# A fused two-layer block on one core: the last steps of the attention and the norms behind it rearranged

## The reference, cut to what matters

```python
def _L1_xattn_ref(x, context, mask, g_norm, null_kv, Wq, Wkv, Wout, g_out):
    ...                      # q, k, v of 16 heads of 64; one null key and value in front
    sim = jnp.einsum('bhid,bhjd->bhij', q, k)
    ...
    attn = jax.nn.softmax(sim.astype(jnp.float32), axis=-1).astype(sim.dtype)
    out = jnp.einsum('bhij,bhjd->bhid', attn, v)
    out = out.transpose(0, 2, 1, 3).reshape(b, -1, INNER)
    out = out @ Wout
    return layer_norm(out, g_out)

def _act_fake_quant(x, clip_factor):
    scale = jax.nn.sigmoid(clip_factor) * jnp.max(jnp.abs(x)) / QMAX
    return jnp.clip(_ste_round(x / scale), -QMAX - 1.0, QMAX) * scale
...
x = x + jnp.tanh(g_xattn[1]) * _L1_xattn_ref(_layernorm(x, axis=-1), ctx_768, ...)
x = x + jnp.tanh(g_ffn[1]) * _L1_ffn_ref(_layernorm(x, axis=-1), L1_ffn_clip_x, ...)
```

## Time and profile before

| what | value |
|---|---|
| time, median of 3 runs | 330.18 us (328.82 to 331.27) |
| the profiled execution: its own time | 329.04 us |
| the profiled execution: its span, first to last instruction | 327.2 us |
| busy in that span: PE, PEld | 301.6 us (92%), 245.2 us (75%) |
| busy in that span: DVE, ACT, POOL | 240.8 us (74%), 230.5 us (70%), 173.9 us (53%) |
| mean granted TensorE clock | 0.99 of full speed |

### The profile page before, as it was taken

The page is one execution under the profiler, slowest core; times in us unless marked ns, Lnnn a source line. Parts: engine busy times, 40 slices in busy tenths (PEclk is TensorE's granted clock), DMA queues, the critical chain, the costliest instruction groups (busy, mean ns, idle before and its releaser), DMA issues.

```text
span 327.2 us, 7975 instructions
## 1 busy us (share of the span) xinstructions
PE 301.6 (92%) x2682; PEld 245.2 (75%) x2682; DVE 240.8 (74%) x723; ACT 230.5 (70%) x781; POOL 173.9 (53%) x301
## 2 busy tenths in 40 slices
PE   6779999999999869999999999999999998977595
PEld 6557668686767658898998988989888777743375
DVE  3887999999885456666777787777777686547865
ACT  2776596969899677877878778787787774319190
POOL 3115616252443145458889797895957849245100
PEclk9999999999999999999999999999999999979989
DMA  5671010002020000000000000000000000000004
GB/s 148 164 205 26 1 26 1 1 2 66 3 62 3 0 0 2 2 2 2 2 3 2 1 4 2 2 0 3 3 2 1 2 3 1 2 0 1 2 0 130
DMA packets 12649, 7.22 MB, mean 22 GB/s; under 512 B 3969, under 2 KB 12161, under 8 KB 12609
## 3 DMA queue, kind: packets, MB, share of 16 engines
q1 hardware_dynamic: 11728, 6.51, 7.2%
q10 hardware_dynamic: 880, 0.20, 0.3%
HBM read 5.66 MB, written 1.05 MB: 20 GB/s over the span
## 4 chain that ended last, share of the span: by engine, by line
PE 73%; DVE 8%; issue 7%; ACT 7%; POOL 4%; DVEq 0%; POOLq 0%; ACTq 0%
PE psum L1084 14%; PE psum L1220 10%; PE psum L1517 9%; PE psum L1531 7%; PE psum L1088 7%; PE psum L1090 6%; PE psum L1089 6%; PE psum L1099 2%; ACT work L1025 2%; DVE hgm L2149 2%; PE psum L1632 2%; PE psum L1540 1%; PE psum L1095 1%; DVE work L2008 1%; PE psum L1317 1%
## 5 line engine op out<-in xcount | busy, mean ns | idle before, releaser
L1025 ACT ACTIVATE work<-psum,nmx 128x129 f32<-128x129 f32 x256 | 83.4, 420 | 25.9 <-DVE nmx L2014 24.8
L603 POOL TENSOR_TENSOR work<-work,rden 128x512 f32<-128x512 f32 x64 | 66.4, 1038 | 0.0
L2014 DVE TENSOR_REDUCE nmx<-psum 128x4 f32<-128x516 f32 x64 | 41.5, 689 | 29.4 <-PE psum L1220 29.3
L1084 PE MATMUL psum<-ident,work 128*128 128x128 f32 (+2 forms) x376 | 58.4, 281 | 3.9 <-DVE work L2008 2.6
L1025 ACT ACTIVATION_READ_ACCUMULATOR work<-psum,nmx 128x1 f32 x256 | 58.7, 229 | 0.0
L1088 PE MATMUL psum<-split 128*128 128x256 f32 (+2 forms) x128 | 52.0, 406 | 1.5 <-issue 0.8
L1084 PEld LDWEIGHTS psum<-ident,work 128*128 128x128 f32 (+2 forms) x376 | 41.7, 142 | 13.1 <-issue 3.3
L2008 DVE COPY work<-psum 128x512 f32<-128x512 f32 x64 | 43.9, 686 | 7.8 <-PE psum L1084 4.9
L1090 PE MATMUL psum<-split 128*128 128x256 f32 (+2 forms) x128 | 43.3, 338 | 0.0
L1089 PE MATMUL psum<-split 128*128 128x256 f32 (+2 forms) x128 | 43.2, 338 | 0.0
L1220 PE MATMUL psum<-KT,work 64*128 64x129 f32 x512 | 37.5, 285 | 2.5 <-DVE den L2024 1.8
(11 more groups left out here) (209 smaller groups left out, 576.6 us busy)
## 6 DMA issues: line engine op xcount, KB each, us to landing
KT<-in_L_xattn_Wkv SPq DMA_DIRECT2D x2, 384.0 KB, 5.2
X<-in_x SPq DMA_DIRECT2D x1, 768.0 KB, 6.8
out_x<-X SPq DMA_DIRECT2D x3, 256.0 KB, 2.3
work<-in_ctx SPq DMA_DIRECT2D x3, 192.0 KB, 2.6
KT<-in_L_xattn_Wout SPq DMA_DIRECT2D x1, 512.0 KB, 4.7
work<-in_L_xattn_Wq SPq DMA_DIRECT2D x1, 512.0 KB, 3.6
work<-in_L_xattn_Wout SPq DMA_DIRECT2D x1, 512.0 KB, 4.0
X<-in_x SPq DMA_DIRECT2D x1, 256.0 KB, 3.3
```

The lines of the kernel that those rows point to most:

```text
L603: pool.tensor_tensor(sx_[:, :, 0:S], sx_[:, :, 0:S], bcast(rden[n % 2][:, :], S), ALU.mult).then_inc(p_ready.sem, 1)
L1025: ins = act.activation(Sx[n % 4][:, j, :], psum[:, here, (j // 2) * K1:(j // 2 + 1) * K1], ACT.Exp, bias=nmx[n % 2][:, j:j + 1], accum_out ...
L1084: return pe.transpose(dst, src, ident[0:m, 0:m])
L2014: dve.tensor_reduce(nmx[n % 2][:, :].rearrange("p (c a) -> p c a", a=2), sim, AX_X, ALU.max, negate=True).then_inc(max_done.sem, 1)
```

## The change

The loops of all four engines now end with round 32 (`NR`), and what is left is written out behind them. Numbers of the steps below are 62 (`NS - 2`) and 63 (`NS - 1`), of the pairs 6 (`NPAIR - 2`) and 7.

- Step 63 is normalised on VectorE (`last_normalise`) in place of GpSimd. It signals with semaphores of its own.
- Its transposes go to bank 6, and ScalarE copies them out (`last_p_evac`); its values go to the second half of bank 0. The copies of the values out of banks 5 and 0 are two (`last_o_evac`), each of half the columns.
- TensorE runs both groups of transposes first, then both halves of `out_proj(30)`.
- The last pair's `y_evac` is gone: `last_statistics` and `last_centred` read bank 7. `last_centred` subtracts the mean and multiplies with the gain in one instruction for each sequence, and `last_output` multiplies with the reciprocal deviation and adds the residual in another.
- On GpSimd `y_affine(6)` stands behind `normalise(62)` in place of before it. On VectorE the next norm of pair 6 stands behind `y_aggregate(7)`, and its maximum behind `x_aggregate(7)`.
- The first run of `keep_clock_long` has 24 matmuls in place of 36.

The core of the diff, with one line of context; the new semaphores and three of the four loop headers are left out:

```diff
...
@@ -364,3 +366,2 @@
         X_STATS_AT, X_AGGR_AT, RSTD_X_AT, XN4_AT, GM_AT = 9, 10, 10, 11, 12
-        LAST = RPP * (NPAIR - 1) + GM_AT
 
@@ -659,8 +660,8 @@
             pool.wait_ge(setup_a.sem, setup_a.at(9))
-            for m in range(LAST + 1):
+            for m in range(NR + 1):
                 if 9 <= m < 21 and m % 2 == 1:
                     down_weights((m - 9) // 2)
-                if in_rounds(m - 1):
-                    normalise(2 * (m - 1))
-                    normalise(2 * (m - 1) + 1)
+                for n in (2 * (m - 1), 2 * (m - 1) + 1):
+                    if 0 <= n < NS - 1:
+                        normalise(n)
                 t = pair_at(m, RSTD_Y_AT)
@@ -668,6 +669,8 @@
                     rstd_y(t)
-                    if t < NPAIR - 1:
+                    if t < NPAIR - 2:
                         y_affine(t)
                 t = pair_at(m, X3_AT)
-                if t is not None and t < NPAIR - 1:
+                if t is not None:
+                    if t == NPAIR - 2:
+                        y_affine(t)
                     y_gain(t)
@@ -680,2 +683,5 @@
                     split_x(t + 2)
+            rstd_x(NPAIR - 2)
+            rstd_y(NPAIR - 1)
+            rstd_x(NPAIR - 1)
 
...
@@ -1045,2 +1051,19 @@
 
+
+            def last_p_evac():
+                act.wait_ge(pt_done.sem, pt_done.at(NS))
+                act.wait_ge(ot_done.sem, ot_done.at(NS - 2))
+                act.activation(PTs[(NS - 1) % 2], bank[6], ACT.Copy).then_inc(pt_last.sem, 1)
+
+            def last_o_evac(h):
+                act.wait_ge(ot_done.sem, ot_done.at(NS - 1 + h))
+                act.wait_ge(wo_done.sem, wo_done.at(NS - 2))
+                act.activation(oT[:, 2 * h * S:2 * (h + 1) * S], bank[(5, 0)[h]][:, 2 * h * S:2 * (h + 1) * S],
+                               ACT.Copy).then_inc(ot_out.sem, 1)
+
+            last_p_evac()
+            pn_evac(NPAIR - 1)
+            last_o_evac(0)
+            last_o_evac(1)
+
             def x_quantised(f):
@@ -1500,7 +1523,11 @@
             def p_transposes(n):
-                pe.wait_ge(p_ready.sem, p_ready.at(n + 1))
-                if n >= 1:
-                    pe.wait_ge(pt_out.sem, pt_out.at(n))
+                if n < NS - 1:
+                    pe.wait_ge(p_ready.sem, p_ready.at(n + 1))
+                    if n >= 1:
+                        pe.wait_ge(pt_out.sem, pt_out.at(n))
+                else:
+                    pe.wait_ge(p_last.sem, p_last.at(1))
+                    pe.wait_ge(q_out.sem, q_out.at(RPP * NPAIR))
                 for j in range(HPU):
-                    ins = transpose(bank[4][:, j * S:(j + 1) * S], Sx[n % 4][:, j, 0:S])
+                    ins = transpose(bank[4 if n < NS - 1 else 6][:, j * S:(j + 1) * S], Sx[n % 4][:, j, 0:S])
                 ins.then_inc(pt_done.sem, 1)
@@ -1510,5 +1537,10 @@
                 b, hg = unit(n)
-                pe.wait_ge(pt_out.sem, pt_out.at(n + 1))
+                if n < NS - 1:
+                    pe.wait_ge(pt_out.sem, pt_out.at(n + 1))
+                else:
+                    pe.wait_ge(pt_last.sem, pt_last.at(1))
                 if n >= 2:
                     pe.wait_ge(ot_out.sem, ot_out.at(n // 2))
+                    if n == NS - 1:
+                        pe.wait_ge(den_done.sem, den_done.at(NS - 1))
                 for j in range(HPU):
@@ -1516,3 +1548,3 @@
                     at = (n % 2) * 2 * S + (j // 2) * S
-                    ins = pe.matmul(bank[5][rows, at:at + S], V[:, b, HPU * hg + j, :],
+                    ins = pe.matmul(bank[5 if n < NS - 1 else 0][rows, at:at + S], V[:, b, HPU * hg + j, :],
                                     PTs[n % 2][:, j * S:(j + 1) * S], start=True, stop=True)
@@ -1522,3 +1554,3 @@
                 t, hg = divmod(m, RPP)
-                pe.wait_ge(ot_out.sem, ot_out.at(m + 1))
+                pe.wait_ge(ot_out.sem, ot_out.at(m + 1 if m < NR - 1 else NR + h))
                 if hg == 0:
@@ -1537,3 +1569,5 @@
 
-                pe.wait_ge(pnr_done.sem, pnr_done.at(UPT * (t + 1)))
+                pe.wait_ge(pnr_done.sem, pnr_done.at(min(UPT * (t + 1), NS - 1)))
+                if t == NPAIR - 1:
+                    pe.wait_ge(pnr_last.sem, pnr_last.at(1))
                 for bb in range(2):
...
@@ -1584,2 +1618,13 @@
                             scores(2 * m + h)
+            p_transposes(NS - 2)
+            p_transposes(NS - 1)
+            for h in range(2):
+                out_proj(NR - 2, h)
+            null_transposes(NPAIR - 1)
+            values(NS - 2)
+            values(NS - 1)
+            null_out(NPAIR - 1)
+            for h in range(2):
+                out_proj(NR - 1, h)
+
             def global_max(n):
@@ -1592,3 +1637,3 @@
 
-            keep_clock_long(bank[6], 36)
+            keep_clock_long(bank[6], 24)
             global_max(0)
@@ -2044,16 +2089,36 @@
 
-            def last_output():
+            def last_normalise():
 
-                t = NPAIR - 1
-                dve.wait_ge(rstdy_done.sem, rstdy_done.at(t + 1))
+                n = NS - 1
+                b, hg = unit(n)
+                dve.wait_ge(rden_done.sem, rden_done.at(n + 1))
+                dve.tensor_tensor(pnr[1][:, b % 2, HPU * hg:HPU * hg + HPU], Sx[n % 4][:, :, S], rden[n % 2][:, :],
+                                  ALU.mult).then_inc(pnr_last.sem, 1)
+                dve.tensor_tensor(Sx[n % 4][:, :, 0:S], Sx[n % 4][:, :, 0:S], bcast(rden[n % 2][:, :], S),
+                                  ALU.mult).then_inc(p_last.sem, 1)
+
+
+            def last_y(bb):
+                return bank[7][:, bb * D:(bb + 1) * D]
+
+            def last_statistics():
+                dve.wait_ge(wo_done.sem, wo_done.at(NS))
                 for bb in range(2):
-                    ins = dve.tensor_scalar(yS[:, bb, :], yS[:, bb, :], mvy[:, bb, 0:1], rstdy[:, bb:bb + 1],
-                                            ALU.subtract, ALU.mult)
-                ins.then_inc(y_norm.sem, 1)
-                dve.wait_ge(y_norm.sem, y_norm.at(t + 1))
-                dve.tensor_tensor(yS, yS, gout_bc[:, :].rearrange("p (o d) -> p o d", o=1).to_broadcast([P, 2, D]),
-                                  ALU.mult).then_inc(yg_done.sem, 1)
-                dve.wait_ge(yg_done.sem, yg_done.at(t + 1))
-                xp = X[:, 2 * t:2 * t + 2, :]
-                dve.tensor_tensor(xp, xp, yS, ALU.add).then_inc(x3_done.sem, 1)
+                    dve.bn_stats(sty[:, bb, :], last_y(bb)).then_inc(y_stats.sem, 1)
+
+            def last_centred():
+                dve.wait_ge(y_aggr.sem, y_aggr.at(2 * NPAIR))
+                dve.wait_ge(x3_done.sem, x3_done.at(NPAIR - 1))
+                for bb in range(2):
+                    dve.scalar_tensor_tensor(out=yS[:, bb, :], in0=last_y(bb), scalar=mvy[:, bb, 0:1], in1=gout_bc[:, :],
+                                             op0=ALU.subtract, op1=ALU.mult).then_inc(y_centred.sem, 1)
+
+            def last_output():
+                dve.wait_ge(rstdy_done.sem, rstdy_done.at(NPAIR))
+                for bb in range(2):
+                    dve.wait_ge(y_centred.sem, y_centred.at(bb + 1))
+                    ins = dve.scalar_tensor_tensor(out=pair_row(NPAIR - 1, bb), in0=yS[:, bb, :],
+                                                   scalar=rstdy[:, bb:bb + 1], in1=pair_row(NPAIR - 1, bb),
+                                                   op0=ALU.mult, op1=ALU.add)
+                ins.then_inc(x3_done.sem, 1)
 
...
@@ -2099,2 +2164,4 @@
                     denominators(2 * (m - 1) + 1)
+                if m == NR:
+                    last_normalise()
                 t = pair_at(m, Y_STATS_AT)
@@ -2104,4 +2171,2 @@
                 if t is not None:
-                    if t == NPAIR - 1:
-                        last_output()
                     x_statistics(t)
@@ -2116,2 +2181,17 @@
                         maxima(2 * m + h)
+            p_evac(NS - 2)
+            x_statistics(NPAIR - 2)
+            x_aggregate(NPAIR - 2)
+            last_statistics()
+            y_aggregate(NPAIR - 1)
+            next_norm(NPAIR - 2, 0)
+            next_norm(NPAIR - 2, 1)
+            last_centred()
+            last_output()
+            x_statistics(NPAIR - 1)
+            x_aggregate(NPAIR - 1)
+            pair_max(NPAIR - 2)
+            for bb in range(2):
+                next_norm(NPAIR - 1, bb)
+            pair_max(NPAIR - 1)
```

More of the change, by code:

```diff
@@ L329, in flamingo_kernel @@
         den_done, rden_done = sig("den_done"), sig("rden_done")
+        pnr_last = sig("pnr_last")
         pnr_done, p_ready = sig("pnr_done"), sig("p_ready")
```

1 line of the change is left out of this document (added).

## The result

The changed kernel took 328.84 us (median of 20 runs, 325.17 to 331.11), the kernel before 330.44 us (20 runs, 328.27 to 333.37). The ratio is 0.992 (0.9895 to 0.9944), 0.8% less. It leaves out the slow runs, those more than 1.5% above the fastest of their kernel, six of the changed kernel's and one of before; the medians of all runs are 1.6 us apart, 0.5%. In a later comparison it was 328.94 against 330.19 us (12 and 23 runs), ratio 0.9975 (0.995 to 1.0), an interval that reaches to no difference. The ratios are those recorded with each comparison and are not exactly the quotients of the medians.

The account below looks back on a forecast made before the run. A chain of waits across engines from 274 to 294 us was taken as the bound. Gains of 1.27 us up to the statistics and 0.78 behind them, about 2.1, give 328.1 from 330.18; stated 328.0, range 326.1 to 329.9 us.

Parts of the forecast that it names:

- Banks and order: Steps 62 and 63 on TensorE: step 63's transposes start 1.07 us earlier, 0.4 given back by the values' end.
- The product on VectorE: Step 63's normalisation: small product 0.18 us, large 128x512 product 0.70 us, taken from VectorE's copy of that shape.
- Reads from PSUM at no cost: Last pair's norm: VectorE reading PSUM directly costs nothing, +0.2 us as upper end; the skill's cycle table gives 0.26.
- From aggregation to residual: Last pair's norm: 1.85 us in place of 2.63, a gain of 0.78, with VectorE last by 0.1 us, not the power.
- Pair 6: Its GpSimd work and VectorE statistics end near 279.1 us, 1.7 us before they would hold up the last pair's.
- The clock: TensorE idles 3.2 us in place of 2.5 ahead of the scale; half-clock cost expected as before, place differing by a microsecond.
- at half for over 5 us: Sign that the forecast is wrong: granted TensorE clock at half for over 5 us behind the scale.
- The first rival: Half clock falls earlier, unread matmuls and input transposes run at full rate: 1.1 us more, 327.0 us; chance 0.20.
- The second: Pair 6's GpSimd work, stretched by more than 1.7 us, holds up the last pair's statistics: 329.1 us; chance 0.06.
- The third: Half clock lasts into the feed-forward products; with 20 of them low, 4.2 us lost, 332.3 us; chance 0.04.

Follow-up runs that it names:

- the run with 2.11: Changed kernel with the banks and the TensorE and ScalarE order of before, one undivided copy of both values: distance from step 63's reciprocal to the scale 11.76 us.
- the filled kernels: Changed kernel with 38 unread matmuls in place of 24 ahead of the first scale, some also 38 in place of 20 ahead of the second: 325.96 to 328.55 us.
- The kernels of 325.96 and 328.94 us: 325.96: changed kernel with 38 unread matmuls ahead of both scales, GpSimd waiting for VectorE's product before pair 6's affine part. 328.94: the changed kernel timed again.

## Why the prediction was right, and where it was not

The forecast was 328.0 us, the same within 1% the likeliest. The median came out at 328.84, and at 0.8% under before by the ratio. By its steps, in us from the end of the reciprocal of step 63:

```
                                    before  forecast  after
transposes of step 62 start           0.43    0.27     0.21
transposes of step 63 start           1.96    0.89     1.02
values end                            4.63    3.97     4.13
projection ends                       6.47    5.62     5.69
statistics start                      6.91    5.64     5.71
last aggregation ends                 7.63    6.37     6.43
residual done (next statistics)      10.28    8.22     8.18
scale starts                         13.17   11.07    11.07
```

The forecast of 11.07 us was met to the hundredth, and that is partly luck: the values end 0.16 us later than forecast, and the later steps make it up. The range was added up loosely: the terms named for its ends give 326.3 and 329.6 us, not 326.1 and 329.9.

- **Banks and order.** Right: 0.94 us for the transposes against 1.07, of which 0.44 are given back by the end of the values, where 0.4 was forecast. The forecast didn't say which of its edits carries this; the experiments do: own banks, order and divided copy 0.69 us of distance, the product's engine 0.30.
- **The product on VectorE.** 0.21 + 0.80 us against 0.18 + 0.70. The copy of the same shape was the right row for the product alone: it took 0.68 and 0.69 us in the two runs in which GpSimd has a wait for it. So the 0.1 us comes from GpSimd's affine part beside it. The chance of a collision was put on GpSimd's side only, at most 0.3 us inside pair 6's slack; VectorE pays as well, and with two-input work beside it 0.62 us (1.30 against 0.68). The Trainium skill ("GPSIMD Engine Reference", Specifications) has the shared SBUF interface that the forecast cited. These rows agree with it.
- **Reads from PSUM at no cost.** Right. Statistics of a pair took 0.50 us from PSUM and 0.49 from SBUF, and the two centrings, which read PSUM, 0.60 us against 0.61 for the two instructions of the same form in `last_output`. By an estimate from the fixed cycles in the Trainium skill ("VectorE: DVE Perf Modes", section on the TRN2 errata) four reads would cost 0.26 us and the gain would be 1.8. The measured one is 2.10, and the norm through SBUF again cost 1.31 us where that estimate gives 0.9, so the traces don't bear it out.
- **From aggregation to residual.** 2.65 before, 1.75 now, forecast 1.85. The power did not stop being last, as the text had it; it still is, by 0.06 us, which is as good as a tie.
- **Pair 6.** The slack of 1.7 us was there to the tenth.
- **The clock.** The step that failed is "I expect the same cost as before". What the forecast calls idle time, 2.5 us before and 3.2 now, holds the small transposes too; TensorE's wait alone was 1.56 us before and 2.04 now. The first scale had one half-rate stretch or none in the two profiles of the changed kernel, and the second two in a row in both (6.9 us each): the sign "at half for over 5 us", though at the other scale. From the second scale on this costs 1.45 us against before by the two profiles (19.33 and 17.88).
- **The gain at equal clock.** What the clock costs also comes out of all runs of before and of the kernels timed repeatedly (131 of them, each with its time and mean clock). A straight line with a level for each kernel gives 0.42 us of time for each us by which the clock, taken over the span, falls short of full. Held at full clock by that slope, before stands at 328.1 us and the changed kernel at 325.9: a gain of 2.1 us (2.14 before rounding), give or take 0.4, which is the forecast's 2.1. At the clocks that they had (0.983 over 46 runs, 0.978 over 32) the means are 330.4 and 328.9, 1.5 us apart. So some 0.6 us of the gain are given back to a lower clock. Whether the shorter run of unread matmuls does that is not shown: filled again (17 runs), the mean is 328.3 and the clock 0.982, and the cut alone, put into the kernel before, gives 330.8 at 0.979; either moves the way that it should, and neither is more than the spread.
- **The first rival** was a matter of the single execution: the profiles of the filled kernels show it each time, and so do three of the nine others. It is worth 0.8 to 1.0 us from the first scale to the second, where 1.1 was forecast. **The second**, pair 6 in the way, has nothing for it in any profile. **The third** (half clock on the path for longer) came at the other scale, and not in the products: half clock ended with the 20 unread matmuls, which hold the first product. It cost the 1.45 us, not the 4.2 of the third rival's sum.

## What to carry to other kernels

Count a chain from an event just ahead of the edit, not from the start: the absolute times of these executions differ by up to 5 us, and the distance repeated to 0.02. Before you give an elementwise product to VectorE, look at what GpSimd does beside it: work with two input tensors cost both sides here, and a wait that takes it out of the way costs nothing as long as it has slack. Where a gap in TensorE's work decides the clock of what follows, judge by the clocks of many runs, fill the gap up to the wait and no further, and compare kernels at equal clock.

## What the runs showed of the hardware

- A 128x512 product on VectorE took 0.68 us with nothing on GpSimd, 0.80 beside GpSimd's affine part (one input tensor, two per-row scalars) and 1.30 beside GpSimd's two-input products. The same affine part of GpSimd took 1.58, 1.66 or 2.11 us, and in the run with 2.11 VectorE's product beside it took only 0.68. Which of the two engines bears the loss therefore changes; what decides it is open.
- Behind an idle time of TensorE of 1.6 to 3.4 us half clock came in most cases and not in all (15 of 19), for 3.4 or 6.8 us; with the same time filled by unread matmuls it came in none of 7. The kernels of 325.96 and 328.94 us differ by 3.0 us, and by only 0.2 in the distance; their mean clocks are 0.996 and 0.979.
- What half clock costs depends on where it falls. 3.4 us of it cost 0.8 to 1.0 us behind the first scale and 0.3 to 0.6 behind the second; 6.8 us there cost 1.7 to 1.9, since the unread matmuls then hold the first product.
- The spread from run to run (325.17 to 331.11 us for the changed kernel) goes in part with each run's granted clock: 0.995 in the fastest, 0.964 in the slowest.
